# Vision-transformer layer on one core: another order of prologue loads, exponentials, softplus, patch turn and output copy

## The reference, cut to what matters

```python
tokens = patchify(x)                                  # (16, 256, 320)
h = layernorm(tokens @ W) * gamma                     # (16, 256, 256)
xn = layernorm(h)
q, k = silu(xn @ Wq), silu(xn @ Wk); v = xn @ Wv      # 16 heads of 64
la = -softplus(xn @ Wa + ba); cum = cumsum(la, axis=1)
decay = exp(where(causal, cum[i] - cum[j], -inf))
o = ((q @ k.T) * decay) @ v
o = groupnorm(o) * gn_w + gn_b                        # per head, over rows and features
h = h + (o * sigmoid(xn @ Wg)) @ Wo
h = h + top2_of_8_experts(layernorm(h))               # router, two layers of each expert, gelu
```

## Time and profile before

| what | value |
|---|---|
| runs | 1316.14, 1318.67, 1321.25 us (median 1318.67) |
| profiled execution | 1316.64 us, its span 1314.6 us |
| granted TensorE clock, mean | 0.986 of full speed |
| busy: PE, ACT, DVE, POOL | 95%, 65%, 63%, 32% of the span |
| one pair in the middle of the attention half | about 100.3 us |

### The profile page before, as it was taken

One profiled execution on the slowest core, in us unless ns is written; L12 is line 12 of the kernel. 1 busy time (PEld: TensorE's weight loads), 2 busy tenths in 40 slices (PEclk: granted clock), 3 DMA queues, 4 the chain that ended last, 5 costly groups with the idle time before them and its releaser, 6 DMA issues. The chain is left out here.

```text
span 1314.6 us, 27299 instructions
## 1 busy us (share of the span) xinstructions
PE 1251.5 (95%) x8534; PEld 1072.4 (82%) x8534; DVE 824.6 (63%) x2120; ACT 858.2 (65%) x2019; POOL 425.4 (32%) x524
## 2 busy tenths in 40 slices
PE   6799999999999999999999999999999999999996
PEld 4576877877877877878878768889899999989996
DVE  4456466566666566665665566657788888555562
ACT  3567567667567567576576465637788888666662
POOL 2111211241241241241241132154445544434433
PEclk8899999999999999999999899999999999999998
DMA  5423222242231341341331335468987886888883
GB/s 185 143 100 90 78 91 88 77 129 74 93 122 55 110 132 49 116 131 47 114 116 56 101 95 193 151 186 245 278 232 220 230 242 184 250 271 269 251 239 83
DMA packets 125607, 194.46 MB, mean 148 GB/s; under 512 B 16272, under 2 KB 91504, under 8 KB 125360
## 3 DMA queue, kind: packets, MB, share of 16 engines
q1 hardware_dynamic: 110864, 175.37, 41.5%
q0 software_dynamic: 13584, 17.26, 6.4%
q10 hardware_dynamic: 1056, 0.55, 0.2%
HBM read 167.40 MB, written 29.05 MB: 149 GB/s over the span
## 5 line engine op out<-in xcount | busy, mean ns | idle before, releaser
L1190 PE MATMUL bank<-xn_sp,big_r 128*128 128x512 f32 x1152 | 315.2, 411 | 2.2 <-DVE big_r L1694 1.7
L1190 PEld LDWEIGHTS bank<-xn_sp,big_r 128*128 128x128 f32 x1152 | 206.6, 190 | 56.4 <-issue 2.4
L837 ACT ACTIVATE dec_x<-dec_x,ncum 128x256 f32<-128x256 f32 (+1 forms) x512 | 189.7, 444 | 10.4 <-POOL dec_x L663 10.4
L1717 DVE TENSOR_TENSOR att<-bank,dec_x 128x384 f32<-128x384 f32 x256 | 130.6, 552 | 102.7 <-PE bank L1229 100.8
L663 POOL TENSOR_SCALAR_AFFINE_SELECT dec_x<-dec_x 128x256 f32<-128x256 f32 x256 | 101.7, 427 | 225.2 <-DMA dec_x<-cum_scratch 224.9
L1535 PE MATMUL bank<-big_r 128*128 128x256 f32 x1296 | 168.0, 286 | 1.9 <-ACT mid_f L907 1.3
L1535 PEld LDWEIGHTS bank<-big_r 128*128 128x128 f32 x1296 | 160.5, 192 | 3.6 <-ACT mid_f L907 1.7
L714 POOL TENSOR_SCALAR mid_f<-mid_f,dec_x 128x256 f32<-128x256 f32 x71 | 77.5, 1096 | 184.7 <-DVE mid_f L1968 182.3
L720 POOL DMA_INDIRECT out<-mid_f,tok x71 | 117.8, 1660 | 53.7 <-POOL mid_f L714 20.2
L1984 DVE TENSOR_TENSOR big_r<-mid_f,big_r 128x256 fp32r<-128x256 f32 x216 | 91.2, 423 | 69.5 <-ACT big_r L927 69.5
L907 ACT ACTIVATE mid_f<-bank,h 128x256 f32<-128x256 f32 x216 | 101.3, 478 | 43.9 <-PE bank L1535 21.6
(11 more groups left out here) (231 smaller groups left out, 2224.5 us busy)
## 6 DMA issues: line engine op xcount, KB each, us to landing
big_f<-in_L_ffn_w SPq DMA_DIRECT2D x68, 1024.0 KB, 6.4
dec_x<-cum_scratch SPq DMA_DIRECT2D x128, 384.0 KB, 3.5
big_w<-in_L_ffn_w SPq DMA_DIRECT2D x12, 1024.0 KB, 6.4
mid_f<-expert_rows SPq DMA_DIRECT2D x27, 261.0 KB, 3.2
h<-h_scratch SPq DMA_DIRECT2D x8, 512.0 KB, 4.6
out<-h SPq DMA_DIRECT2D x16, 256.0 KB, 4.0
xt<-in_x SPq DMA_DIRECT2D x15, 256.0 KB, 3.8
h_scratch<-h SPq DMA_DIRECT2D x15, 256.0 KB, 2.6
```

The costliest lines, as they stand in the source:

```text
L837: act.activation(d, d, ACT.Exp, bias=ncum[p % 2][:, NS * u + s, 2 * c + hh:2 * c + hh + 1]).then_inc(M["exp_done"], 1)
L1190: mm = pe.matmul(bank[target][:, :], wp[:, k, c * P:(c + 1) * P], xp[:, k, :], start=(k == 0 and j == 0), stop=(k == EC - 1 and j == 2))
L1717: dve.tensor_tensor(att[hh][:, :], bank[4 + hh][:, 0:LW], dec[n % RING][:, hh, :], ALU.mult).then_inc(M["mult_done"], 1)
```

## The change

It has five parts. (1) SP waits for the token weight, ACT's constants and both first images before it issues the loads of Wq and Wv. (2) In ACT's prologue list `weight_hi(3)` moves ahead of `softplus(0)`, `tanh_k` and `tanh_g` go ahead of both `decay` calls, the first `keep_v` goes ahead of `keep_cum`, and the two `scaled_h` go behind `tanh_g(0,0)`. Image 1 gets its `h` and `xn` in `h2` and `xn2`, so `keep_v` no longer waits for the stores. PE's `cum(0)` and `cum_rows(0)` move forward by one `values` or two; DVE's `weight_lo(2)` goes behind `silu_q(0,0)`. SP's list keeps its order of stores. (3) In each pair at c = 5, `softplus(p+1)` goes behind `tanh_k` and `decay(p,6,1)`. (4) At c = 1 PE's `turn(2p+2)` goes behind `gates`, and ACT's `keep_xnT(2p+2)` and `scaled_h(2p+2)` behind `tanh_g`. (5) At c = 7 ACT's `keep_o(p,6)` goes ahead of `xn_hi(p+1)` and `y_hi(p,0,0)`.

```diff
-        side_h = [h1, mid_f[:, 2816:3328].rearrange("p (s n) -> p s n", s=NS)]
-        side_n = [xn1, mid_f[:, 3328:3840].rearrange("p (s n) -> p s n", s=NS)]
+        side_h = [h1, h2[:, 0:NS, :]]
+        side_n = [xn1, xn2[:, 0:NS, 0:E]]
...
             load_patches(0)
             load_patches(1)
+            sp.wait_ge(M["wt_in"], 32)
+            sp.wait_ge(M["c_in"], 64)
+            sp.wait_ge(M["xt_in1"], 32)
             load_weight(0)
             load_weight(1)
             load_patches(2)
...
                 if p == 0 and t >= NS and n == 0:
                     act.wait_ge(M["tok_ps"], 2)
-                    act.wait_ge(M["h_out"], 32)
...
             def last_step(p):
                 main, nxt = pair(p), pair(p + 1)
+                if main:
+                    keep_o(p, 6)
                 if nxt:
                     xn_hi(p + 1)
                 if main:
                     y_hi(p, 0, 0)
-                    keep_o(p, 6)
...
-                if c == 5 and nxt:
-                    softplus(p + 1)
                 if c == 6 and main:
                     affined(p, 0, 0)
                 if main:
...
                     decay(p, c + 1, 1)
                     if c in (1, 2):
                         keep_v(p, c + 4, 0)
+                if c == 5 and nxt:
+                    softplus(p + 1)
...
-                if c == 1 and nxt:
-                    keep_xnT(2 * p + 2)
-                    scaled_h(2 * p + 2)
...
                 if main:
                     tanh_g(p, c + 1)
+                if c == 1 and nxt:
+                    keep_xnT(2 * p + 2)
+                    scaled_h(2 * p + 2)
...
             xn_hi(0)
+            weight_hi(3)
             softplus(0)
+            tanh_q(0, 0)
+            keep_v(0, 0, 2)
+            keep_cum(0)
+            for i in range(1, TP):
+                keep_v(0, i, 2 + i)
+            tanh_k(0, 0)
+            tanh_g(0, 0)
             scaled_h(0)
             scaled_h(1)
-            tanh_q(0, 0)
-            keep_cum(0)
-            weight_hi(3)
-            for i in range(TP):
-                keep_v(0, i, 2 + i)
             decay(0, 0, 0)
-            tanh_k(0, 0)
-            tanh_g(0, 0)
             decay(0, 0, 1)
...
-                if c == 1 and nxt:
-                    turn(2 * p + 2)
                 if c == 1 and main:
                     values(p, 5, 0, "sq_done", NP * p + 3)
...
                 if main:
                     gates(p, c + 1)
+                if c == 1 and nxt:
+                    turn(2 * p + 2)
...
             queries(0, 0)
+            cum(0)
             values(0, 0, 2, "s1_xnT", 2)
+            cum_rows(0)
             values(0, 1, 3, "s1_xnT", 2)
-            cum(0)
             values(0, 2, 4, "s1_xnT", 2)
-            cum_rows(0)
...
             log_decay(0)
-            weight_lo(2)
             running_sums(0)
             silu_q(0, 0)
+            weight_lo(2)
             weight_lo(3)
```

More of the change, by code:

```diff
@@ L166, in vit_layer @@
         xs = sb("xs", [P, EC, SP2])
-        h2 = sb("h2", [P, TP, E])
-        xn2 = sb("xn2", [P, TP, EW])
         cumT = sb("cumT", [TP * H, P])
@@ L183, in vit_layer @@
         pick = sb("pick", [P, TP, TOPK, X])
+        h2 = sb("h2", [P, TP, E])
+        xn2 = sb("xn2", [P, TP, EW])
         side_x = [xt, mid_f[:, 2048:2048 + (KT + 1) * S].rearrange("p (k n) -> p k n", k=KT + 1)]
-        side_h = [h1, mid_f[:, 2816:3328].rearrange("p (s n) -> p s n", s=NS)]
-        side_n = [xn1, mid_f[:, 3328:3840].rearrange("p (s n) -> p s n", s=NS)]
+        side_h = [h1, h2[:, 0:NS, :]]
+        side_n = [xn1, xn2[:, 0:NS, 0:E]]
         little = pick[:, :, :, :].rearrange("p t k n -> p (t k n)")
```

## The result

The changed kernel is slower: 1330.96 us (median of 1327.55, 1333.92, 1332.01 and 1329.91) against 1319.58 us before, a ratio of 1.0089 [1.0056, 1.0122]. That is 11.4 us, or 0.9%, where +2.5 us was forecast, and above the range. The profiled execution took 1327.55 us, with a span of 1325.5 us, against 1316.64 and 1314.6: +10.9 us. Its mean granted clock is 0.980 (before 0.986). The profile is that of the fastest of the four runs; the others took 2.4 to 6.4 us more, and no profile shows where.

What follows compares the result with a forecast made beforehand. TensorE, busy for 95% of the span, was taken as the bound, so only its waits count. The terms +5.5 - 0.9 - 2.1 - 1.1 - 3.9 + 3.0 + 2.0 gave +2.5 us, 1318.67 to 1321.2 us, range 1314 to 1329.

Steps and rivals of the forecast that it cites:

- the clock: Behind the new wait in pairs 1 to 6, the granted clock falls once in six pairs: +2.0 us, bounds 0 to +12.
- under both: Argument against a fall at route: the new 1.45 us wait is shorter than both 1.55 us (no fall) and 1.95 us (fall).
- Rival (A): The clock falls at route in four to six of pairs 1 to 6: 1327 to 1331 us, slower; chance 0.20.
- Softplus's block and its neighbours: On ACT, softplus starts 1.88 us after tanh_k, takes 3.41 us, keep_x2 follows tanh_g by 0.95: net +5.5 us over pairs 1 to 6.
- rival (C): Each table load costs a second one's time in softplus's new place: 15 us, 1336 us, slower; chance 0.04.
- The 17 us: By the skill's 1.38 us drain per table load, softplus's block would be 2.8 us longer and the sum 17 us higher.
- Where PE waits: In pairs 1 to 6, PE newly waits 1.45 us at route for keep_x2, and gains 0.53 us at the late scores.
- Output copy: keep_o(6) first at c = 7: -2.1 us in pairs 1 to 5, -1.1 in pair 0, -3.9 in pair 6, 0 in pair 7.
- End of pair 0: In pair 0, softplus moved later gives -0.9 us and the earlier output copy -1.1 us.
- Turn: Turn and its copies at c = 1: PE did not wait there, so 0 us, bounds 0 and +3.
- Prologue: Before the first weighted: earlier loads, but store_cum behind store_h leaves PE idle about 10 us, then half clock; +3.0 us, bounds 0 to +5.5.
- The expert half: The half after attention is not touched by the change and was moved as a whole.

Runs made afterwards that it cites:

- e5: The changed kernel with the moved softplus, turn and output copy undone, leaving the prologue alone: 1318.13 us, ratio 1.0005 to the kernel before.
- e1: The kernel before with only softplus moved behind tanh_k and the exponentials: 1339.45 us, ratio 1.0162.
- e3: The kernel before with only keep_o(p,6) moved ahead of xn_hi and y_hi: 1311.99 us, ratio 0.9935.
- e12: The changed kernel with route(2p-2), eight small matmuls, moved behind weighted(6,0): 1331.93 us, ratio 1.0084 to the kernel before.
- e8: The kernel before with only turn(2p+2) and ACT's two copies moved later at c = 1: 1318.13 us, ratio 1.0007.
- e9: The changed kernel with keys(7) computed an extra time ahead of cum in pairs 1 to 6: 1317.23 us, ratio 1.0000 to the kernel before.
- e10: The changed kernel with softplus back in its old place and store_cum(0) and load_decay ahead of both store_h: 1300.28 us, ratio 0.9859 to the kernel before.
- e2: e1 with keys(7) computed an extra time ahead of cum in pairs 1 to 6: 1321.97 us, ratio 1.0032 to the kernel before.
- e11: The changed kernel, softplus still late, with keep_x2 and keep_o(p,5) ahead of it and store_cum first: 1306.2 us, ratio 0.9909 to the kernel before.

## Why the prediction was wrong

**The step that failed is the clock.** The prediction put the wait at 1.45 us "nearest by length" to a wait of 1.55 us without a fall, and took one fall in six pairs, +2.0 us. The profile shows five, of 3.4, 3.4, 6.8, 3.4 and 3.4 us: 4 x 1.5 + 3.1 = 9.1 us. That is 7.1 us above the +2.0, of the 8.4 by which the profiled execution (+10.9) passed the forecast (+2.5). Its price for one fall, 2 us, was near enough (1.5); how often it falls was not. The error of method: a single wait of 1.55 us, in one execution and with another load of work on PE around it, was read as a bound. And the wait came out at 1.66 us, above that bound and below the 1.95 us behind which a fall was known, so even by the prediction's own rows "under both" held only for the wait that it had worked out. Rival (A), 1327 to 1331 with a chance of 0.20, is what happened, but for the place of the wait.

The rest, by the prediction's own steps:

- *Softplus's block and its neighbours:* right in order and size (1.88, 3.41 and 0.97 us of ACT, against 1.88, 3.41 and 0.95). `ACT_TABLE_LOAD` takes 1.28 us, and `tanh_g` starts at 517.70, 0.02 us after the second one ended. The Trainium skill, ScalarE: Activation LUTs, "What ACT_TABLE_LOAD costs", has a drain on top of the load; by that rule this trace disagrees in the new place as in the old one, and rival (C) is out. The 17 us that the prediction put beside it counted a longer block in the new place alone; it would have been as long in the old place, ahead of the scores, and the sum would have moved by less.
- *Where PE waits:* wrong place. `cum`, which writes bank 6, waits for the copy that empties it, and stands ahead of `route`; I had read the copy only as `route`'s input. As `cum` comes earlier, the wait is 1.66 us and not 1.45. With the two gains of 0.53 and 0.42 a pair without a fall comes to +0.71 by sum and +0.73 by the marks; predicted were +0.5.
- *Output copy:* right: -6.3 us alone against -7.1, with the gain of pair 6 as described. In pair 7 `weighted(7,7,0)` waits 0.61 and not 1.55 us, `weighted(7,7,1)` 0.74 us where it did not wait: won and lost again, as predicted. In the changed kernel the clock falls in pair 6 all the same, but at the new wait; without the 1.5 us of that fall the stretch from mark 7 comes to -2.7, predicted were 0.9 - 3.9 = -3.0.
- *End of pair 0:* -1.7 us, predicted -2.0. *Turn:* 0, right.
- *Prologue:* right in mechanism: `store_cum` behind `store_h`, idle for about 10 us (10.76), half clock behind it. It came earlier than I had it, though: statistics at 11.46 us, queries at 25.83 and not 27.45, `store_cum` at 40.32 and not 43.2, `weighted` at 51.22 and not 53.6. By the first mark it is +1.4 us (+1.9 in e5), all of it the longer half clock; the sum was +3.0, and alone it measured +0.6 [-2.0, +3.3].
- *The expert half* was moved as a whole and came out 1.0 us longer, within what it varies by from one of these profiles to the next, with identical instructions: from the last `weighted` on 485.8 to 494.1 us. The three longest (e1 and e3 492.9, e12 494.1) wait longer for the loads of the routed rows, 7.5 to 8.9 us in all against 3.7 to 6.4 in the others, and the clock falls in the middle of it for 3.4, 3.4 and 10.2 us; but for 3.4 us it falls in some of the shorter ones too (e5, e8, e9). Waits of PE in it, before and e1:

```profile
PE bank L1307 <- DMA mid_f<-expert_rows: 5.4, 5, 1.9
```

```profile
PE bank L1307 <- DMA mid_f<-expert_rows: 8.9, 5, 2.4
```

What makes these loads late in some kernels no run here shows.

**The parts add up where they act.** By the medians they give +21.2 (e1), -6.3 (e3), +0.6 (e5) and +0.6 (e8), together 16, against 11.4 for the change. By the profiles, up to the last `weighted` of pair 7, they give +16.5, -7.9, +1.3 and +0.1, together +10.0, and the change +9.9. So they do not disturb each other there, as far as one profile of each can tell; the rest of the mismatch lies in the expert half and in the scatter of the runs.

**What stays open:** which waits bring the clock down. Behind the same wait of about 1.95 us before `weighted(7,1,0)` (762.00 in the earlier trace rows) it fell in the profiles of the kernel before and of the changed one, not in those of e3 (1.94), e10 (1.96) and e12 (1.95); pair 1's 1.66 us had no fall in three profiles (the changed kernel, e1, e12), pairs 2 to 6 had one each time, and 0.61 us had one once. The runs show that filling the gap ends it, and not what else PE must have done around it.

## What to carry to other kernels

Where TensorE is busy for 95% of the time, price a new wait at its length plus the fall of the clock that it may bring (here 1.5 to 3.1 us, behind 1.66 us of waiting), and take a short wait that once went unpunished as no bound. Moving a long block later in an in-order list helps its old follower and delays each of its new ones: list them all, with each buffer that they free as well as each result that they hand on, and move those ahead of it, or leave it. In a queue of transfers put the store that the next stage waits for ahead of the ones that nobody needs soon; that was worth 10.6 us here, more than any of the five parts gained.

## What the runs showed of the hardware that I had not expected

- More work can be faster: 36 surplus matmuls, 9 us of TensorE's time, in six waits of 1.66 us took 13.7 us (e9) and 17.5 us (e2) off the kernel, as the granted clock then stays at 1.00.
- Falls of 3.4 or 6.8 us at half clock came behind waits of only 1.66 us in five of six pairs of three kernels (the changed one, e1 and e12), and once behind 0.61 us (e11).
- Stretches with identical instructions are not equally long from one kernel to the next: the expert half varied by 8.3 us (485.8 to 494.1 over fourteen profiles), more than most of the terms that this study was about. In the longest ones TensorE waits for the same loads for up to 8.9 us in all, in the others for as little as 3.7.
